# First attention of a two-block gated network: the output projection as three rounded products from the fifth tile on, and its transposes ahead of the second score half

## What is computed

```python
def _L0_xattn_ref(q, k, v, w_q, b_q, w_k, b_k, w_v, b_v, w_o, b_o):
    qh = _split(q @ w_q + b_q, B, L)          # 16 heads of 16 columns
    kh = _split(k @ w_k + b_k, B, L)
    vh = _split(v @ w_v + b_v, B, L)
    ...                                       # softmax(qh kh^T * 0.25) vh
    return out @ w_o + b_o
x = x + jnp.tanh(g_xattn[0]) * _L0_xattn_ref(_layernorm(x), ctx_1024, ctx_1024, ...)
x = x + jnp.tanh(g_ffn[0]) * _L0_ffn_ref(_layernorm(x), ...)   # router: 8 experts, 2 of them per row
```

## Time and profile before

| | us |
|---|---|
| median of three runs | 1317.04 |
| lowest and highest | 1316.01, 1319.75 |
| the profiled execution | 1309.47 |
| its span in the trace | 1307.7 |
| TensorE matmuls busy | 1261.9 (96%) |
| VectorE busy | 886.5 (68%) |
| ScalarE busy | 796.7 (61%) |
| GpSimd busy | 747.4 (57%) |

### The profile page before, as it was taken

The page is one execution under the profiler, slowest core; times in us unless marked ns, Lnnn a source line. Parts: engine busy times, 40 slices in busy tenths (PEclk is TensorE's granted clock), DMA queues, the critical chain, the costliest instruction groups (busy, mean ns, idle before and its releaser), DMA issues.

```text
span 1307.7 us, 38200 instructions
## 1 busy us (share of the span) xinstructions
PE 1261.9 (96%) x14755; PEld 1129.1 (86%) x14755; DVE 886.5 (68%) x2362; ACT 796.7 (61%) x1739; POOL 747.4 (57%) x835
## 2 busy tenths in 40 slices
PE   9999999998999999999999988999999999999797
PEld 8898888886999999999999967899999998655476
DVE  5878888876765566555664048999999997321387
ACT  5676676664777777777775446666666665323454
POOL 2578888754777877778784044566666643000231
PEclk9999999999999999999999999999999999999999
DMA  6675564633767777777777611621111111699812
GB/s 226 230 249 181 196 206 168 220 135 121 246 211 239 218 223 217 231 231 220 219 224 261 264 45 54 241 92 52 53 51 58 52 34 38 276 427 427 299 62 69
DMA packets 103891, 237.51 MB, mean 182 GB/s; under 512 B 8992, under 2 KB 86176, under 8 KB 91296
## 3 DMA queue, kind: packets, MB, share of 16 engines
q1 hardware_dynamic: 97568, 218.29, 48.5%
q0 software_dynamic: 6144, 16.79, 4.0%
HBM read 174.22 MB, written 60.82 MB: 180 GB/s over the span
## 4 chain that ended last, share of the span: by engine, by line
PE 88%; DVE 5%; DMA 3%; issue 2%; ACT 2%; POOL 0%; SPq 0%; DVEq 0%; ACTq 0%; PEldq 0%; POOLq 0%
PE ps L2127 13%; PE psT L2112 7%; PE ps L703 6%; PE psS L680 5%; PE ps L1073 5%; PE psT L689 4%; PE ps L1015 4%; PE ps L2112 3%; PE psS L2112 3%; PE ps L998 2%; PE ps L1032 2%; PE ps L942 2%; PE psT L695 2%; DMA arena<-wset_dram 2%; PE ps L714 2%
## 5 line engine op out<-in xcount | busy, mean ns | idle before, releaser
L2080 POOL TENSOR_TENSOR wb_lo<-arena,wb_hi 128x2048 fp32r<-128x2048 f32 x64 | 297.7, 4652 | 93.5 <-ACT wb_hi L2203 93.5
L2127 PE MATMUL ps<-wb_hi,hT_hi 128*128 128x256 f32 x528 | 151.7, 287 | 2.4 <-DVE hT_lo L2256 2.4
L689 PE MATMUL psT<-arena 32*128 32x128 f32 x2048 | 148.5, 283 | 0.4 <-ACT arena L1245 0.4
L2127 PE MATMUL ps<-wb_lo,hT_hi 128*128 128x256 f32 x528 | 147.7, 280 | 0.0
L2127 PE MATMUL ps<-wb_hi,hT_lo 128*128 128x256 f32 x528 | 147.7, 280 | 0.0
L680 PE MATMUL psS<-arena 32*128 32x256 f32 x1024 | 138.2, 387 | 0.8 <-ACT arena L1322 0.4
L2203 ACT CAST wb_hi<-arena 128x1024 fp32r<-128x1024 f32 x128 | 130.7, 1045 | 8.2 <-DMA arena<-w_dram 8.0
L689 PEld LDWEIGHTS psT<-arena 32*128 32x128 f32 x2048 | 124.1, 186 | 1.1 <-issue 0.6
L1689 POOL TENSOR_TENSOR arena<-arena,eps_sb 128x1 f32<-128x1 f32 x94 | 23.5, 250 | 146.2 <-DVE arena L1560 104.6
L2268 DVE TENSOR_TENSOR arena<-ps,arena 128x512 f32<-128x512 f32 (+1 forms) x39 | 25.4, 650 | 117.1 <-PE ps L2127 76.6
L1702 POOL DMA_INDIRECT arena<-xs_rows,slot_i x64 | 64.3, 1005 | 69.4 <-DMA xs_rows<-arena 54.3
(11 more groups left out here) (508 smaller groups left out, 3861.3 us busy)
## 6 DMA issues: line engine op xcount, KB each, us to landing
arena<-wset_dram SPq DMA_DIRECT2D x24, 2048.0 KB, 16.0
xs_rows<-arena SPq DMA_DIRECT2D x33, 1024.0 KB, 5.5
arena<-w_dram SPq DMA_DIRECT2D x32, 1028.0 KB, 5.9
arena<-w_dram SPq DMA_DIRECT2D x32, 1024.0 KB, 5.9
arena<-w_dram SPq DMA_DIRECT2D x7, 2052.0 KB, 13.7
w_sb<-xs_rows SPq DMA_DIRECT2D x33, 256.0 KB, 2.7
xs_rows<-arena SPq DMA_DIRECT2D x33, 256.0 KB, 5.5
arena<-ctxT_dram SPq DMA_DIRECT2D x63, 128.0 KB, 2.8
```

Source lines behind the costliest of these rows:

```text
L689: nc.tensor.matmul(psT[:, b, j * P:(j + 1) * P], kbd_[p, (k - 1) % NK, c, par, :], qT[p, (k - 1) % 3, c, :], start=j == 0, stop=False, ski ...
L2080: nc.gpsimd.tensor_tensor(wb_lo[:, u % 2, part], wb_raw[:, u % 2, part], wb_hi[:, u % 2, part], ALU.subtract).then_inc(w_g.sem, 1)
L2127: last = nc.tensor.matmul(ps[5][:, t * D:(t + 1) * D], hp[:, f, t * P:(t + 1) * P], wp[:, f, :], start=f == 0 and t == 0 and n == 0, stop= ...
```

## The change

From the fifth tile on (`wide_first = 4`), the output projection of the first attention is the sum of three products in the rounded type. `wo_wide` is split once, in step 4: ScalarE writes `wide_hi`, GpSimd writes `wide_lo`. In every step from 6 on, ScalarE's copy of the transposed `att` writes the rounded `aT_hi`, and a new VectorE instruction, ahead of the second reduction of the maxima, writes `aT_rest`, the difference. The two matmuls of 264 columns become six. Separately, in every step from 2 on, the two transposes of `att` move from behind the second score half to ahead of it, and ScalarE's copy of them moves ahead of the residual rows.

```diff
         lbase = carve(1)
         place[0] = max(place[0], attention_used)
         stash_near = carve(4, 2 * D)
+        wide_at = place[0]
         yb = carve(2, 2, D)
+        place[0] = attention_end - D
+        assert place[0] >= wide_at + 2 * C * (D + E0) + C * P
         zero = carve(D)
...
+        wide_hi, wide_lo = (rounded(f"wide_{part}", wide_at + n * C * (D + E0), C, D + E0) for n, part in enumerate(("hi", "lo")))
+        aT_rest = rounded("aT_rest", wide_at + 2 * C * (D + E0), C, P)
...
-                    if not A and valid(k - 2):
+                    if valid(k - 2):
                         pe.wait_ge(out_v.sem, out_v.at(k - 2, "att"))
                         for c in range(C):
                             last = nc.tensor.transpose(ps[7][:, c * P:(c + 1) * P],
...
-                    if A and valid(k - 2):
-                        pe.wait_ge(out_v.sem, out_v.at(k - 2, "att"))
-                        for c in range(C):
-                            last = nc.tensor.transpose(ps[7][:, c * P:(c + 1) * P],
-                                                       att[:, c * HC:(c + 1) * HC, :].rearrange("p h d -> p (h d)"), cv["ident"])
-                        last.then_inc(o_p.sem, 1)
...
-                        if A:
+                        if A and k - 2 < wide_first:
                             for c in range(C):
                                 last = nc.tensor.matmul(ps[7][:, 0:D + E0], aT[:, c, :], wo_wide[:, c, :],
                                                         start=c == 0, stop=c == C - 1)
+                        elif A:
+                            if k - 2 == wide_first:
+                                pe.wait_ge(lo_g.sem, lo_g.at(0, "wide"))
+                            pe.wait_ge(aT_v.sem, aT_v.at(k - 2, "lo"))
+                            last = thrice(ps[7][:, 0:D + E0], (aT_hi, aT_rest), (wide_hi, wide_lo))
...
+                    if A and k == 4:
+                        act.wait_ge(ld_w, 32)
+                        act.wait_ge(fold_v, 4)
+                        nc.scalar.copy(wide_hi[:, :, :], wo_wide).then_inc(hi_a.sem, 1)
...
-                    if not A and valid(k - 2):
+                    if valid(k - 2):
                         act.wait_ge(o_p.sem, o_p.at(k - 2, "aT"))
                         before(act, o_p.sem, o_p.at(k - 3, "O"))
...
                     if A and k < B:
                         residual_rows(k - 3)
-                    if A and valid(k - 2):
-                        act.wait_ge(o_p.sem, o_p.at(k - 2, "aT"))
-                        before(act, o_p.sem, o_p.at(k - 3, "O"))
-                        nc.scalar.copy(aT, ps[7][:, 0:D].rearrange("p (c t) -> p c t", c=C)).then_inc(av_a.sem, 1)
...
-                    if not A and valid(out_i):
+                    if valid(out_i) and (not A or out_i >= wide_first):
                         dve.wait_ge(av_a.sem, av_a.at(out_i, "aT"))
                         before(dve, o_p.sem, o_p.at(out_i - 1, "O"))
-                        nc.vector.tensor_tensor(aT_lo[:, :, :], ps[7][:, 0:D].rearrange("p (c t) -> p c t", c=C),
+                        nc.vector.tensor_tensor((aT_rest if A else aT_lo)[:, :, :], ps[7][:, 0:D].rearrange("p (c t) -> p c t", c=C),
                                                 aT_hi[:, :, :], ALU.subtract).then_inc(aT_v.sem, 1)
...
+                    if A and k == 4:
+                        pool.wait_ge(hi_a.sem, hi_a.at(0, "wide"))
+                        nc.gpsimd.tensor_tensor(wide_lo[:, :, :], wo_wide, wide_hi[:, :, :], ALU.subtract).then_inc(lo_g.sem, 1)
```

More of the change, by code:

```diff
@@ L386, in build @@
         rest_v, rest_g = sem("rest_v"), sem("rest_g")
-        hi_a, lo_g = track("hi_a", "k0 v0 o1 v1 dv", 1), track("lo_g", "k0 v0 o1 v1 dv", 1)
+        hi_a, lo_g = track("hi_a", "k0 v0 wide o1 v1 dv", 1), track("lo_g", "k0 v0 wide o1 v1 dv", 1)
         ld_prep, ld_set, ld_slots = sem("ld_prep"), [sem(f"ld_set{i}") for i in range(SETS)], sem("ld_slots")
@@ L567, in attention @@
             kbd_, NK = (kbd_ring, 4) if A else (kbd, 3)
-            aT_v = Track(rest_v, ["lo"], B)
+            wide_first = 4
+            aT_v = Track(rest_v, ["lo"], B, -wide_first if A else B - wide_first)
             ctx_g = Track(rest_g, ["hi", "lo"], B, -2 * ctx_first if A else 2 * (B - 4) - 2 * ctx_first)
@@ L1283, in scalar @@
                         nc.scalar.copy(xT.rearrange("p c t -> p (c t)"), ps[5][:, 0:D]).then_inc(pre_a.sem, 1)
-                    if not A and valid(k - 2):
+                    if valid(k - 2):
                         act.wait_ge(o_p.sem, o_p.at(k - 2, "aT"))
                         before(act, o_p.sem, o_p.at(k - 3, "O"))
-                        if not A:
+                        if not A or k - 3 >= wide_first:
                             before(act, aT_v.sem, aT_v.at(k - 3, "lo"))
-                        nc.scalar.copy(aT if A else aT_hi[:, :, :], ps[7][:, 0:D].rearrange("p (c t) -> p c t", c=C))\
-                            .then_inc(av_a.sem, 1)
+                        nc.scalar.copy(aT if A and k - 2 < wide_first else aT_hi[:, :, :],
+                                       ps[7][:, 0:D].rearrange("p (c t) -> p c t", c=C)).then_inc(av_a.sem, 1)
                     if not A and k == B:
```

## The result

The changed kernel took 1327.56 us (median of 6 runs, 1325.29 to 1331.31), the kernel before 1316.95 us (median of 6, 1312.73 to 1319.75). The ratio is 1.0081, with a 95% interval of 1.0058 to 1.0103: 10.6 us slower. In a later session ten runs of the changed kernel and 31 of the kernel before gave 1.0070 (1.0043 to 1.0097). I had forecast +9.6 us.

A forecast was written before the change was run, and what follows sets the result against it. VectorE's chain from the second reduction to the matmul of the maxima was taken as the bound. Terms 0.27 + 0.9 + 0 + 0.1 + 2.5 + 6.0 + 0.27 - 0.45 = +9.6 us gave 1326.6 us, range 1320.5 to 1335.5.

The forecast's parts named there:

- What bounds the kernel: At the matmul of the maxima, TensorE's and VectorE's chains end together in 17 of 27 steps; VectorE's longer once changed.
- The products: Output projection: six matmuls in 0.79 us against 0.98, 0.19 us less TensorE work per tile, not on the path.
- The transposes: Ahead of the second score half, every step from 2: scores 0.27 us later, even steps +0.19 us, 2.5 us in thirteen.
- R: Start of VectorE's second reduction before the change, when the last scores are complete; both chains are timed from it.
- The subtraction in odd steps: Waits for ScalarE's copy behind four key activations, second reduction at R + 0.63: +0.50 us per step, 6.0 us in twelve.
- Rival 3: Odd steps: VectorE's last split waits for GpSimd's long subtraction, +1.23 us instead of +0.50, 1335.4 us in all; chance 0.10.
- The start: Steps 2 to 5: +0.27, +0.9 (transposes wait for `att` in step 3), nothing and +0.1 us.
- the 1.18 us stall of step 4: TensorE's own loss behind the start of the reduction in step 4, taken to cover the shift there, so zero cost.
- The end: Step 31 +0.27 us; step 32 -0.45 us, bounds -0.9 and +0.3; last tile's subtraction offsets the projection's saving, zero.
- the earlier exponential: Step 32: ScalarE's exponential no longer queues behind the copy of the transposes, which delay the scores; taken as -0.45 us.
- The sum: Whole kernel: all terms together +9.6 us on the median of 1317.0, giving 1326.6 us, 0.7% slower.

The follow-up runs named there:

- the control: Kernel before the change, with the whole values' matmul group moved ahead of the matmul of the maxima, float32 products and transposes behind kept: 1317.16 us, ratio 1.0006.

## Why the prediction was right, step by step

**What bounds the kernel.** Two chains that end together at the matmul of the maxima, and VectorE's becoming the longer one: shown. Each part alone slows the kernel (1.0047 and 1.0068), and cover put back in the place takes the whole loss away (0.9994). "VectorE's chain is longer in every step" is too strong: it holds for odd steps and for even steps with a long L1623. In even steps with a short one (3 of the 11 from 8 to 28 in the first profile, none in the second) TensorE's own matmuls come last or just as late, and the step costs nothing.

**The products.** I took 0.19 us per tile off TensorE's work; the control gives 0.15. Against the forecast of 0.79 us for the six matmuls 0.90 was measured, and 1.07 against 0.98 for the float32 pair, as another group follows there. That it would not show in the time: right.

**The transposes.** I took 0.27 us. In the new place the scores begin 0.54 us behind the last product of the values (213.72 to 214.26 in the changed kernel) where it was 0.32 before (209.06 to 209.38): 0.22. With a long L1623 L1066 comes at R + 0.22 + 2.64 = R + 2.86, where the terms make R + 0.27 + 2.66 = R + 2.93; with a short one at R + 0.22 + 2.39 = R + 2.61, where they make R + 2.68. The forecast took the mean of the two kinds, R + 2.84. Measured in the even steps 8 to 28, it is R + 2.79 in the first profile (8 long of 11) and R + 2.86 in the second (11 of 11): +0.14 and +0.21 against the +0.19 taken. Both kinds were put 0.07 us too late, and that the second profile comes so close is luck, since its steps were all of the long kind.

**The subtraction in odd steps.** The reduction was forecast at R + 0.63, and it is R + 0.22 + 0.41 = R + 0.63. L1066 follows 2.45 us behind, at R + 3.08, inside 3.04 to 3.29: +0.43 instead of the +0.50 taken, since L1623 was short in every odd step. Two steps grew by 0.58 and 0.65 us in the two profiles, where 0.69 was forecast. Tile 5 to 31 grew by 6.9 and 7.7 us, where the terms make 2.5 + 6.0 + 0.27 = 8.8.

**Rival 3**, GpSimd's long subtraction: it stands at 208.83 and L1623 at 208.84 in the odd step above, and L1623 still took 0.15. In 11 odd steps of each of the two profiles L1623 starts 0.009 to 0.014 us behind it, and it is held in none. So "rival 3 follows whenever L1716 gets ahead" is wrong by the start times of the profile; that the rival did not come was a matter of hundredths, and so partly luck. The smaller part of it happened: L1611 took 0.41 us instead of 0.17 and L1619 0.28 instead of 0.17, the latter beside the shorter GpSimd instruction; together they put L1623 0.06 us later.

The reading behind it was incomplete too. The prediction has L1618 long "where GpSimd's L1714 ran beside it". In the odd step of before, where L1618 was short, L1714 ran beside it as well and started first:

```profile
203.92 0.46 POOL L1714 TENSOR_SCALAR ctx_pair_hi<-arena 128x256 fp32r<-128x256 f32 x1
203.96 0.15 DVE L1618 TENSOR_TENSOR m<-arena,m 128x16 bf16<-128x16 f32 x1
```

Here GpSimd's instruction took 0.46 us instead of 0.41. Which of the two is held up goes by a few thousandths of a microsecond; the counts are in the last section.

**The start.** The shift of step 3 was as forecast (its reduction 1.14 us later against that of step 2; 1.04 forecast). But I let the 1.18 us stall of step 4 stand. It isn't in the changed kernel's traces, nor in the second trace of before. From tile 2 to tile 5 it is 28.09 and 28.08 us with the change, and 28.08 and 26.66 without. So the start costs nothing against one profile of before and 1.4 us against the other; my terms for the steps 2 to 5 made 1.27.

**The end.** The term with the wrong sign. I had -0.45 us; from tile 31 to the last slot indices it takes 21.25 and 20.83 us instead of 19.99 in both profiles of before, +1.3 and +0.8. The projection in step 32 waits for the subtraction (0.4 us), and in both traces the granted clock was 0.5 for 3.4 us in that stretch, which it was not in either trace of before. The two kernels with early transposes and no subtraction have neither the low clock there nor the longer end (19.95 and 19.91). So the transposes don't make it; how much is the subtraction's and how much the clock's is open. Nor did the earlier exponential give the 0.45 us.

**The sum.** Attention: +9.6 forecast. Start to end it is +8.4 and +8.7 us against the first profile of before, +6.7 and +7.0 against the second, which took 3.2 us more ahead of tile 2, with its 6.8 us at half the clock, and 1.4 less behind it. The time: +10.6 us in the first session, +9.2 in the second. The 0.5 to 3.9 us between attention and time aren't settled. The stretch behind the attention goes with the number of held VectorE instructions (995.8 to 1011.1 us), and no run shows whether the change alters how often these come. So that the measured 1327.56 lies within 1 us of the forecast is partly luck: the mechanism and the size of its terms are shown in the steps, the last 1 to 3 us are not.

## What to carry to other kernels

An engine that is busy all the time can still have slack in a place: read, at each wait, how long the other chain is from the point where both begin. Work that stands between a producer's last result and the wait for its consumer is cover; making it shorter, or moving it ahead of that result, turns it into a wait once the slack of the place is used up (0.3 us in the odd step of the earlier trace rows, less in the even one). The remedy is to put other work of known length ahead of that wait, a whole group rather than a part of one, before judging whether the shorter work was worth having.

## What the runs showed of the hardware that I had not expected

- Six rounded matmuls of 264 columns save 0.15 us per tile against the float32 pair (0.90 us instead of 1.07, each from its start to the group behind), not a factor: that is 0.15 us for a rounded matmul and 0.53 for a float32 one, and the rounded form needs three times as many.
- Behind a group of matmuls with 32 weight columns the next weight load came 0.2 us late (5.2 us in 26 steps), whether scores or the matmul of the maxima followed. Splitting such a group costs that once more. It is not these groups alone: behind the two early transposes the loads came 0.17 us late, and behind the float32 projection those of the values' group up to 0.34 in the control (9.0 us in 26 steps).
- A VectorE instruction on 6 to 48 columns lasted 4.1 to 4.6 us beside a GpSimd subtraction of 2048 columns. How many were held differed from one execution of the same kernel to the next (three and one), and a stall of up to 10.9 us on TensorE followed.
- Which of two small instructions is held is decided in a few thousandths of a microsecond, and not quite by the start times in the profile. Over all 14 traces VectorE's last split (128x16) began 0.028 to 0.037 us behind GpSimd's rounding of the context in 52 steps: it took 0.15 or 0.16 us each time, and GpSimd's 0.45 or 0.46. It began 0.042 to 0.050 behind in 119 steps: it took 0.40 each time, and GpSimd's 0.41. Between 0.038 and 0.041 both came (52 held, 22 not). Each held split cost 0.25 us of the whole in a step where VectorE's chain decides.
- Ninety-five runs of one kernel spread over 21 us, with mean granted clocks of 0.988 to 0.999. A fitted line gives about 1.6 us for each 0.001 of clock. A change of under 5 us can be read from the steps of a trace long before the times show it.
